# Edge pass of a graph network on one core: destination side by one-hot matmul from products in SBUF

## What is computed

```python
i, j = (edge_index[0], edge_index[1])
x_i = x[i]
x_j = x[j]
out_i = act(jnp.concatenate([x_i, edge_attr], -1) @ W).reshape(-1, HEADS, DIM)
out_j = act(jnp.concatenate([x_j, edge_attr], -1) @ W).reshape(-1, HEADS, DIM)
alpha = act((jnp.concatenate([out_i, out_j], -1) * att).sum(-1))
...
alpha = segment_softmax(alpha, i, N_NODES)
msg = out_j * alpha[:, :, None]
aggr = jax.ops.segment_sum(msg, i, num_segments=N_NODES)
```

## Time and profile before

| | us |
|---|---|
| runs, median (range) | 15665.35 (15663.43 to 15672.95) |
| profiled execution, own time | 15684.04 |
| its span | 15682.3 |
| TensorE's granted clock, mean of full speed | 0.64 |
| busy, share of the span | PE 45%, DVE 46%, ACT 28%, POOL 65% |
| `edge_pass`, first gather to last scatter | 320.65 to 6768.20 |
| `edge_softmax` | 6779.3 to about 7415 |

### The profile page before, as it was taken

The page is one execution under the profiler, slowest core; times in us unless marked ns, Lnnn a source line. Parts: engine busy times, 40 slices in busy tenths (PEclk is TensorE's granted clock), DMA queues, the critical chain, the costliest instruction groups (busy, mean ns, idle before and its releaser), DMA issues. The chain is left out here.

```text
span 15682.3 us, 142629 instructions
## 1 busy us (share of the span) xinstructions
PE 7119.8 (45%) x27704; PEld 5207.8 (33%) x27704; DVE 7155.3 (46%) x13864; ACT 4381.7 (28%) x7904; POOL 10134.6 (65%) x9676
## 2 busy tenths in 40 slices
PE   5444444444444444410455309943333553333377
PEld 4333333333333333310355303333333333333233
DVE  6666666666666666655577500122222222222301
ACT  0555555455554455510466400100000000000000
POOL 1777777777777777738777770067777357777500
PEclk9677777677676677655566559655555555555588
DMA  1544444444444444480466408411111221111155
GB/s 41 130 128 129 129 130 130 129 130 129 129 130 129 129 129 129 129 47 9 135 183 181 128 3 296 182 45 26 26 26 26 72 62 25 25 26 25 18 195 211
DMA packets 867764, 1601.13 MB, mean 102 GB/s; under 512 B 510485, under 2 KB 518653, under 8 KB 817264
## 3 DMA queue, kind: packets, MB, share of 16 engines
q1 hardware_dynamic: 536176, 1173.07, 24.6%
q0 software_dynamic: 331392, 426.19, 11.7%
HBM read 1091.51 MB, written 505.30 MB: 102 GB/s over the span
## 5 line engine op out<-in xcount | busy, mean ns | idle before, releaser
L1377 POOL DMA_INDIRECT l2s_got<-rel_d,l2s_idx x3232 | 3232.8, 1000 | 2141.9 <-POOLq L1374 1244.0
L1403 PE MATMUL l2s_ps<-l2s_got,l2s_oh 128*128 128x65 f32 (+1 forms) x6464 | 1473.2, 421 | 2782.1 <-PEq L1401 2782.1
L1403 PEld LDWEIGHTS l2s_ps<-l2s_got,l2s_oh 128*128 128x128 f32 x6464 | 1408.9, 330 | 2849.1 <-issue 2849.1
L1096 POOL DMA_INDIRECT count_d<-all_list_val,all_list_idx x1568 | 1807.4, 1153 | 502.6 <-issue 462.6
L623 POOL DMA_INDIRECT edge_gath<-h_d,edge_idx_d x1576 | 1688.6, 1071 | 480.6 <-issue 480.6
L619 POOL DMA_INDIRECT edge_gath<-h_d,edge_idx_s x1576 | 1671.6, 1061 | 480.4 <-issue 390.8
L1078 DVE TENSOR_TENSOR net_acc<-net_acc,l2s_ps 128x65 f32 (+1 forms) x3232 | 719.8, 223 | 2721.1 <-DVEq L1425 1845.7
L631 POOL DMA_INDIRECT rows_d<-edge_rows,edge_place x1576 | 1646.1, 1044 | 480.6 <-issue 480.3
L766 DVE SCALAR_TENSOR_TENSOR edge_rows<-edge_z,edge_soft 128x1024 f32<-128x1024 f32 x784 | 952.2, 1215 | 2008.5 <-DVEq L764 2008.4
L699 PE MATMUL edge_z<-edge_w_i,edge_in_i 128*128 128x256 f32 x3140 | 1361.1, 524 | 763.9 <-PEq L728 451.0
L692 PE MATMUL edge_tp<-all_ident,edge_gath 128*128 128x128 f32 x1576 | 428.6, 428 | 1924.8 <-DMA edge_gath<-h_d,edge_idx_d 1641.5
(11 more groups left out here) (340 smaller groups left out, 11941.5 us busy)
## 6 DMA issues: line engine op xcount, KB each, us to landing
at_rows<-rows_d SPq DMA_DIRECT2D x444, 528.0 KB
count_d<-edge_zero SPq DMA_DIRECT2D x196, 1024.0 KB
edge_srow<-in_src SPq DMA_DIRECT2D x197, 512.0 KB, 5.1
edge_lrow<-lo_d SPq DMA_DIRECT2D x197, 512.0 KB, 6.1
l1s_cnt<-count_d SPq DMA_DIRECT2D x49, 1600.0 KB, 6.6
l3s_cnt<-count_d SPq DMA_DIRECT2D x49, 1600.0 KB, 6.5
rel_d<-l2t_out SPq DMA_DIRECT2D x100, 768.0 KB, 3.2
l1s_cnt<-count_d SPq DMA_DIRECT2D x49, 1536.0 KB, 6.5
```

Of the source, the lines that this page charges most:

```text
L1096: pool.indirect_dma_start(out=cells, out_offset=bass.IndirectOffsetOnAxis(ap=net.list_idx[i][:, k:k + 1], axis=0), in_=net.list_val[i][:, ...
L1377: pool.indirect_dma_start(out=got[r][:, j, 0:cols], out_offset=None, in_=table, in_offset=bass.IndirectOffsetOnAxis(ap=idx[i][:, k:k + 1], ...
L1403: ins = pe.matmul(ps[q][:, j, 0:wide], oh[q][:, j, :], got[r][:, j, 0:wide], start=True, stop=True)
```

## The change

`edge_pass` runs over the 1616 items, 202 groups of 8, rather than over the 1568 tiles. All edges of an item that counts are in one destination block; edges of its tile that belong to another block get the row number NU = 6272 and up, so that their rows go to spare places. The item lists are made by a new block `dst_items` ahead of the pass, no longer in `edge_softmax`, which loses that part. A new block `node_products` computes `h @ W[0:64]` for all 49 blocks of nodes and leaves it in SBUF (`products`).

In a group POOL then gathers by source only: 8 gathers, two tiles turned per transpose. The destination side becomes a matmul of a one-hot (`oh_dstT`, 128 by 128 per item) with the block's `products`, read at an offset held in a register; the edge features are added by a second matmul into the same PSUM. The source side is computed turned (`z_i`, weights stationary, 512 edges moving), and its product with `att` is taken by PE (`dots`: 16 matmuls of 2 columns) instead of DVE. `z_i` and `z_j` have one buffer each, `at` too.

```diff
-            def turn(q):
-                for half in TWO:
-                    s.wait_ge(turned, 1).then_inc(turned, -1)
-                    cols = bass.ds(half * 4 * P, 4 * P)
-                    s.copy(in_i[q][0:D, cols], tp[0:D, :, :].rearrange("p j e -> p (j e)"))
-                    s.copy(in_j[q][D:2 * D, cols], tp[D:2 * D, :, :].rearrange("p j e -> p (j e)")
-                           ).then_inc(in_ready, 1)
...
             with Loop(nc, s, GROUPS) as it:
                 for q in TWO:
+                    save(0)
+                    s.wait_ge(zi_ready, 1).then_inc(zi_ready, -1)
+                    softplus_tail(soft_i[:, :], zi, soft_i_ready, 1, 2)
                     ids((it * 2 + q + 2) * G, q)
...
+                    save(3)
+                    s.wait_ge(zj_ready, 1).then_inc(zj_ready, -1)
+                    softplus_tail(soft_j[:, :], zj, soft_j_ready, 4)
+                    save(5)
+                    s.wait_ge(zi_ready, 1).then_inc(zi_ready, -1)
+                    softplus_tail(soft_i[:, :], zi, soft_i_ready, 6, 7)
                     turn(1 - q)
+                    s.wait_ge(zj_ready, 1).then_inc(zj_ready, -1)
+                    s.sem_inc(feats_free, 1)
+                    softplus_tail(soft_j[:, :], zj, soft_j_ready)
...
+            def outs_i(q, half):
+                for c in TWO:
+                    ins = pe.matmul(z_i[:, c, :], w[:, c * P:(c + 1) * P],
+                                    feats[q][:, half * HP:(half + 1) * HP], start=True, stop=True)
+                ins.then_inc(zi_ready, 1)
+
+            def outs_j(q, half, blocks):
+                pe.wait_ge(zj_free, 1).then_inc(zj_free, -1)
+                for i in range(HALF):
+                    j = half * HALF + i
+                    with Scratch(nc, pe):
+                        pe.matmul(z_j[:, i, :], oh_dstT[q][:, j * P:(j + 1) * P], products[:, bass.ds(blocks[j], OUTJ)],
+                                  start=True, stop=False)
+                    ins = pe.matmul(z_j[:, i, :], feats[q][D:2 * D, j * P:(j + 1) * P], w[D:2 * D, :], start=False,
+                                    stop=True)
+                ins.then_inc(zj_ready, 1)
+
+            def dots(half):
+                pe.wait_ge(zi_free, 1).then_inc(zi_free, -1)
+                for i in range(HALF):
+                    for c in TWO:
+                        ins = pe.matmul(dots_i[:, half * HALF + i, 2 * c:2 * c + 2], out_i[:, c, i * P:(i + 1) * P],
+                                        att_i[:, c, :], start=True, stop=True)
+                if half:
+                    ins.then_inc(dots_ready, 1)
...
+                    pe.wait_ge(feats_loaded[q], 16 * G).then_inc(feats_loaded[q], -16 * G)
+                    pe.wait_ge(feats_ready, 1).then_inc(feats_ready, -1)
+                    outs_i(q, 0)
+                    pe.wait_ge(blocks_listed, 1).then_inc(blocks_listed, -1)
+                    blocks = item_values(nc, pe, item[q][0:1, 1, :], (NBU - 1) * OUTJ)
+                    pe.sem_inc(blocks_free, 1)
+                    running(q, 0)
+                    running(q, 1)
+                    pe.wait_ge(dst_onehot, 1).then_inc(dst_onehot, -1)
+                    outs_j(q, 0, blocks)
+                    for j in (2, 3, 4):
+                        running(q, j)
+                    dots(0)
+                    outs_i(q, 1)
+                    running(q, 5)
+                    outs_j(q, 1, blocks)
+                    free_values(nc, blocks)
+                    running(q, 6)
+                    running(q, 7)
+                    turn(1 - q, it * (16 * G) + 16 * G * (1 + q))
+                    dots(1)
...
+                    out_of_i()
+                    ranks(q, 0)
+                    v.wait_ge(scattered[q], it * (16 * G) + (16 * G if q else 16))
+                    out_of_j(q, 0)
+                    out_of_i()
                     v.wait_ge(at_ready, 1).then_inc(at_ready, -1)
...
+                    ranks(q, 1).then_inc(ranked, 1)
+                    v.wait_ge(ranked, 1).then_inc(ranked, -1)
+                    v.sem_inc(ids_free, 1)
+                    dst_hot(1 - q)
+                    src_hots(w0 + G, 1 - q)
...
+                    out_of_j(q, 1)
```

More of the change, by code:

```diff
@@ L321, in _ @@
[L321 to L328 removed]
+                done(v.tensor_copy(lead[:, :], raw[1][:, :, 0]))
@@ new lines, in _ @@
+                done(v.tensor_scalar(bound[:, :], net.iota[0:TC, 0:NB], float(P), None, ALU.mult))
+                done(v.tensor_tensor(below[:, :, :], lead[:, None, :].to_broadcast([TC, NB, KC]),
+                                     bound[:, :].unsqueeze(2).to_broadcast([TC, NB, KC]), ALU.is_lt))
+                v.tensor_reduce(count[:, :], below[:, :, :], AX.X, ALU.add).then_inc(counted, 1)
+                for i, (k0, some) in enumerate(chunks):
+                    v.wait_ge(turned, i + 1)
+                    ins = v.tensor_copy(src_u[:, k0 * TC:(k0 + some) * TC].rearrange("p (k c) -> p k c", k=some),
+                                        tp[i % 2][:, 0:some, 0:TC]).then_inc(copied, 1)
@@ L344, in count_dst_blocks_vector @@
[L344 to L352 removed]
+                v.wait_ge(summed, 1)
@@ new lines, in softplus_tail @@
+            def softplus_tail(soft, z, ready, j=None, last=None):
+                s.activation(soft, z, ACT.Abs).then_inc(abs_made, 1)
+                if j is not None:
+                    save(j)
+                s.wait_ge(abs_made, 1).then_inc(abs_made, -1)
+                s.activation(soft, soft, ACT.Exp, scale=-1.0).then_inc(exp_made, 1)
+                if last is not None:
+                    save(last)
+                s.wait_ge(exp_made, 1).then_inc(exp_made, -1)
+                s.activation(soft, soft, ACT.Ln, bias=1.0).then_inc(ready, 1)
@@ L663, in _ @@
+            zi, zj = z_i[:, :, :].rearrange("p c e -> p (c e)"), z_j[:, :, :].rearrange("p t f -> p (t f)")
             ids(0, 0)
             ids(G, 1)
+            for k in TWO:
+                s.activation(upto[k][:, NBU:NB], net.part[:, :], ACT.Copy, bias=float(EP))
             turn(0)
@@ new lines, in ranks, with out_of_i @@
+            def ranks(q, half):
+                for j in range(half * HALF, (half + 1) * HALF):
+                    ins = v.scalar_tensor_tensor(
+                        junk_r[:, j, :], srow[q][:, j * P:(j + 1) * P], src_g[q][:, j:j + 1],
+                        before[:, :], ALU.is_equal, ALU.mult, accum_out=rank[:, j:j + 1])
+                return ins
+            def out_of_i():
+                v.wait_ge(soft_i_ready, 1).then_inc(soft_i_ready, -1)
+                v.scalar_tensor_tensor(out_i[:, :, :], z_i[:, :, :], 0.0,
+                                       soft_i[:, :].rearrange("p (c e) -> p c e", c=2),
+                                       ALU.max, ALU.add).then_inc(zi_free, 1)
@@ L1783, in build @@
         with Mem(nc, "edge") as e:
-            index_lists(net, m, e)
-            histogram_src(net, e)
+            net.start_src = e.sb("start_src", [P, NB])
+            net.first = e.sb("first", [P, NBU])
+            with Mem(nc, "lists") as lists:
+                index_lists(net, e, lists)
+                histogram_src(net, e)
+            dst_items(net, m, e)
             source_items(net, m, e)
+            node_products(net, e)
             net.retire()
```

609 lines of the change are left out of this document (335 added, 274 removed).

## The result

The changed kernel takes 16895.28 us (median of 4 runs, 16855.94 to 16917.56) against 15669.15 for the kernel before (4 runs, 15663.43 to 15678.0). The ratio is 1.0783, 95% interval 1.0770 to 1.0796. The profiled execution has a span of 16914.5 us, 1232 more than before; the forecast was 1000 less.

The account below looks back on a forecast made before the run. POOL was taken to bound the kernel before, and waits between TensorE, ScalarE and VectorE the changed one. Edge pass -1106, softmax -64, new blocks +170 give -1000 from 15684.0; less 18.7, 14665 us, range 14050 to 15550.

Parts of the forecast that it names:

- the price of `outs_j`: In the edge pass, each float32 matmul of 256 columns was taken at 0.52 us at full rate, 0.85 at half.
- the loop stays at full rate: In the edge pass, dense matmul work keeps TensorE at 2.4 GHz, with a mean clock of 0.9 or more.
- The circle: In the edge pass, waits between TensorE, ScalarE and VectorE set the group: 24.4 us, with handovers and a detour 26.3.
- the rival's factor: In the edge pass, TensorE at half rate takes 0.85 / 0.52 = 1.63 times as long.
- The slower rival: In the whole edge pass loop, TensorE runs at half rate: 37.6 us a group, 16950 us; chance 0.11.
- POOL: In the edge pass, POOL falls from 32.9 to about 22 us a group and waits some 4 for VectorE's rows.
- SP: In the edge pass, SP issues 12 DMAs of some 0.5 us a group, has 26 us, and delays nobody.
- Softmax: In the softmax stage, the first compare on loaded columns comes about 132 us after its start; the stage saves 64.
- New blocks: Ahead of the pass, `dst_items` adds 115 us and `node_products` 55, together 170, with nothing hiding them.

Follow-up runs that it names:

- zj_full_k: The changed kernel with the second matmul of each `outs_j` tile over all 128 rows, against a copy of W with zeroed upper rows: 14871.32 us, ratio 0.9492.

## Why the prediction was wrong

- **The step that failed is the price of `outs_j`** ("one float32 matmul of 256 columns starts 0.51 us after the one before; I take 0.52"). The row behind it is of pairs that both have 128 rows. The new pair has 128 and 64, and 16 calls a group took 0.63 at full rate and 1.15 at half. At full rate that is 1.8 us a group; at half rate, which held for four fifths of the time (a mean of 0.59 between 0.50 and 1.00), 9.2 a half group where 6.8 would have come out of 0.85.
- **Its consequence was the clock.** "By that the loop stays at full rate" failed: 0.59, with TensorE 90% busy. I had argued from idle stretches alone. The Trainium skill's rule (TensorE: Matmul & The Clock Gate, Loop structure matters more than you think), that dense matmul work keeps the clock up and long waits lose it, would give the full rate here, where TensorE was 90% busy and its longest wait 1.4 us; the trace differs from it, with 0.59. The runs put in its place: exposed loads (0.59 to 0.78 when gone), then short idle times (0.78 to 0.84), and not the dots. The repair of `outs_j` took 37.47 - 27.32 = 10.2 us a group off, of the 11.2 that the forecast had missed. The loads' own time is 16 x 0.20 to 0.30 = 3.2 to 4.8 us of it, so the larger part was the clock, a term at which the forecast had put nothing.
- **The circle was mis-sized less.** With the loads hidden a group takes 27.32 us at clock 0.78, for 26.3 forecast at 1.00. That it comes so near is partly luck, since two errors nearly cancel: the rate was lower than forecast, and some prices were too high, dots 0.22 a call at full rate (1.74 for 8, for 0.30) and 256 columns 0.43 (for 0.52). The 0.51 was read from the first call behind a running count, which is longer (0.68 against 0.59 for the next). 512 columns at half rate took 1.78, for 1.70 by the rival's factor. zj_full_k came to 14871 us, the forecast was 14665.
- **The slower rival** said 37.6 us a group and 16950 us; it was 37.47 and 16895. Its place was right, TensorE at half rate as the bound. Its sum was partly luck: it had 0.85 for `outs_j` (1.15 measured) and 0.49 for a call of dots (0.42), and took the half rate for the whole time (four fifths). Its chance of 0.11 looks too low in hindsight: the row that spoke for it, 0.50 in a window 90% busy, was explained away.
- **POOL** left the bound as said, with 3409 us of waiting for VectorE's rows, 17 us a group and not 4. **SP** held nobody up.
- **Softmax**: the first compare comes 130.5 us after the start (132 forecast). **New blocks**: 156.6 for 170. The row of DVE for it:

```profile
8219.04 2.94 DVE L1147 TENSOR_TENSOR sm_keep_f<-sm_al 128x1567 f32<-128x1567 f32 x1 [130.39 <-DMA sm_bet<-in_beta]
```

## What to carry to other kernels

Price a matmul from a row whose neighbours have the same rows as the new ones will have, not only the same columns: here padding 64 rows with zeros, more work on paper, took 12% off the time. When an engine becomes the bound, its clock is a term of the sum with a price of its own (here some 0.34 us a group of 37 for 0.01), and a busy share of 90% is no proof of a high rate. Before dropping a change that came out slower, look whether its new bound has one cheap fault: the same idea was 7.8% slower as written, 5.1% faster with that fault mended, and 7.6% faster with the products split in bf16 parts besides.

## What was not expected of the hardware

- A float32 weight load is hidden beneath the matmul before it where both have 128 rows or both 64, and is exposed where 128 and 64 alternate: 0.30 us a call at half rate (1.15 - 0.85), 0.20 at full (0.63 - 0.43).
- A stream 98% busy stayed at 1.2 GHz for 10 us, and the exposed loads, not the many short dots, went with that; once at the full rate, the same loads did not lower it.
- In three sessions of five all kernels lost time with three engines idle at once, and a group took 34 to 39 us whatever TensorE did. The chip alone is not the reason, since one of them was slow in one session and not in another; what is stays open.
